# The first half of the first adjacency tile comes in two transfers of 256 columns, and one short warm-up matmul stands where two stood

## The reference, cut to what matters

```
def reference(x, adj, L0_gnn_W, L0_gnn_b):        # x (4096, 256), adj (4096, 4096), W (256, 256)
    h = jnp.maximum(_layernorm(x, axis=-1), 0.0)
    agg = jnp.matmul(adj, h)
    out = jnp.matmul(agg, W.T) + b
    return x + jax.nn.relu(out)
```

## Time and profile before

| | |
|---|---|
| median of 3 runs | 380.52 us (380.36 to 380.57) |
| the profiled execution's own time | 380.32 us |
| its span, first to last instruction | 378.5 us |
| TensorE busy | 375.0 us, 99% of the span |
| VectorE busy | 212.8 us, 56% |
| ScalarE busy | 180.8 us, 48% |
| GpSimd busy | 47.3 us, 13% |
| DMA | 80.25 MB, mean 212 GB/s |

### The profile page before, as it was taken

One profiled execution on the slowest core, in us unless ns is written; L12 is line 12 of the kernel. 1 busy time (PEld: TensorE's weight loads), 2 busy tenths in 40 slices (PEclk: granted clock), 3 DMA queues, 4 the chain that ended last, 5 costly groups with the idle time before them and its releaser, 6 DMA issues.

```text
span 378.5 us, 4516 instructions
## 1 busy us (share of the span) xinstructions
PE 375.0 (99%) x1650; PEld 308.4 (81%) x1650; DVE 212.8 (56%) x295; ACT 180.8 (48%) x227; POOL 47.3 (13%) x88
## 2 busy tenths in 40 slices
PE   9999999999999999999999999999999999999997
PEld 5888888888888888888888888888888888888885
DVE  5999988886444444565564535444464444444424
ACT  4878776765343434543643343434355243434341
POOL 4576732321000000001001000000000100000000
PEclk9999999999999999999999999999999999999999
DMA  7999887658655665556866856565656775656203
GB/s 265 345 314 301 253 300 243 206 193 299 202 192 198 177 210 185 203 175 213 290 207 208 293 178 207 177 208 182 203 187 193 258 240 197 185 204 184 95 2 111
DMA packets 22774, 80.25 MB, mean 212 GB/s; under 512 B 2496, under 2 KB 2880, under 8 KB 22752
## 3 DMA queue, kind: packets, MB, share of 16 engines
q1 hardware_dynamic: 19584, 68.30, 54.5%
q0 software_dynamic: 3168, 11.67, 8.9%
HBM read 75.76 MB, written 4.19 MB: 211 GB/s over the span
## 4 chain that ended last, share of the span: by engine, by line
PE 99%; DVE 0%; issue 0%
PE bank L443 92%; PE bank L486 6%; PE bank L499 1%; DVE out_sb L340 0%
## 5 line engine op out<-in xcount | busy, mean ns | idle before, releaser
L443 PE MATMUL bank<-adj_hi,h_sb 128*128 128x512 f32 x1024 | 254.7, 389 | 0.0
L246 DVE TENSOR_TENSOR adj_lo<-adj_in,adj_hi 128x1024 fp32r<-128x1024 f32 x126 | 154.5, 1226 | 144.2 <-ACT adj_hi L361 144.2
L443 PEld LDWEIGHTS bank<-adj_hi,h_sb 128*128 128x128 f32 x1024 | 192.3, 188 | 40.0 <-ACT h_sb L371 0.3
L361 ACT ACTIVATE adj_hi<-adj_in 128x1024 fp32r<-128x1024 f32 x126 | 133.5, 1060 | 175.9 <-PE bank L443 172.9
L443 PE MATMUL bank<-adj_lo,h_sb 128*128 128x512 f32 x512 | 137.8, 389 | 0.0
L443 PEld LDWEIGHTS bank<-adj_lo,h_sb 128*128 128x128 f32 x512 | 96.1, 188 | 20.0
L238 POOL DMA_DIRECT2D out_t_dram<-out_sb x3 | 2.2, 726 | 205.5 <-DVE out_sb L340 205.5
L220 POOL TENSOR_TENSOR rstd<-var_eps,minus_half 128x1 f32<-128x1 f32 x32 | 27.3, 853 | 4.5 <-DVE var_eps L271 1.9
L371 ACT ACTIVATE h_sb<-centred,rstd 128x256 fp32r<-128x256 f32 x32 | 15.9, 497 | 3.4 <-POOL rstd L220 3.1
L381 ACT ACTIVATE centred<-x_sb,neg_mean 128x256 f32<-128x256 f32 x31 | 15.5, 499 | 3.1 <-DVE neg_mean L286 2.2
L292 DVE SCALAR_TENSOR_TENSOR h_sb<-centred,rstd,h_sb 128x256 fp32r<-128x256 f32 x32 | 15.3, 477 | 0.0
(11 more groups left out here) (26 smaller groups left out, 42.8 us busy)
## 6 DMA issues: line engine op xcount, KB each, us to landing
adj_in<-adj_t_dram SPq DMA_DIRECT2D x126, 512.0 KB, 4.1
xt_sb<-x_t_dram POOLq DMA_DIRECT2D x4, 1024.0 KB, 7.6
x_sb<-x_dram POOLq DMA_DIRECT2D x7, 512.0 KB, 7.1
out_t_dram<-out_sb POOLq DMA_DIRECT2D x3, 1024.0 KB, 4.9
adj_in<-adj_t_dram SPq DMA_DIRECT2D x4, 256.0 KB, 4.5
out_t_dram<-out_sb SPq DMA_DIRECT2D x3, 256.0 KB, 2.0
x_sb<-x_dram POOLq DMA_DIRECT2D x3, 128.0 KB, 6.0
w_sb<-w_t_dram POOLq DMA_DIRECT2D x1, 256.0 KB, 6.6
```

Of the source, the lines that this page charges most:

```text
L246: nc.vector.tensor_tensor(adj_lo[:, k, :], adj_in[:, k, :], adj_hi[:, k, :].bitcast(fp32), ALU.subtract).then_inc(s_lo, 1)
L361: nc.scalar.activation(adj_hi[:, k, :], adj_in[:, k, :], ACT.Copy).then_inc(s_hi, 1)
L443: last = nc.tensor.matmul(bank(g, kb, c)[:], h_sb[:, t, hp, kb * P:(kb + 1) * P], adj_parts[ap][:, n % U, chunk(c)], start=(t == 0 and (hp ...
```

## The change

The first chunk of unit 0, 512 columns, is loaded by two transfers of 256 columns, each with its own semaphore (`s_q`), so the first transfer of adjacency has rows of 1 KB in place of 2 KB, and SyncE issues one transfer more before all that follow. VectorE rounds each quarter of the unit when it has landed. TensorE takes the first pass of the first chunk in four matmuls of 256 columns in place of two of 512, the first two of them when the first quarter has been rounded (`s_quarter`). The second rounded quarter raises the same semaphore `s_hi` that the whole rounded chunk raised before, so ScalarE and VectorE's next steps wait as they did. The two warm-up matmuls of 256 columns behind the first landing become one of 128 columns.

```diff
+    HALF = BANK // 2
+    QUARTERS = (slice(0, HALF), slice(HALF, BANK))
-    WARM_ON = 2
+    WARM_ON = 1
...
             load_x(sp, 0)
-            load_chunk(0, 0)
+            g, t = UNITS[0]
+            for i, cols in enumerate(QUARTERS):
+                at = g * GW + cols.start
+                sp.dma_start(adj_in[:, 0, cols], adj_v[:, t, at:at + HALF]).then_inc(s_q[i], 16)
             load_chunk(0, 1)
...
             def first_rounded():
-                dve.wait_ge(s_early[0][0], 16)
-                nc.vector.tensor_copy(adj_hi[:, 0, chunk(0)], adj_in[:, 0, chunk(0)]).then_inc(s_hi, 1)
+                for i, (cols, made) in enumerate(zip(QUARTERS, (s_quarter, s_hi))):
+                    dve.wait_ge(s_q[i], 16)
+                    nc.vector.tensor_copy(adj_hi[:, 0, cols], adj_in[:, 0, cols]).then_inc(made, 1)
...
+            def first_sums(cols):
+                for kb in range(KB):
+                    nc.tensor.matmul(bank(0, kb, 0)[:, cols], h_sb[:, 0, 0, kb * P:(kb + 1) * P],
+                                     adj_hi[:, 0, cols], start=(cols.start == 0), stop=False,
+                                     skip_group_check=True)
...
                 pe.wait_ge(s_hhi, 1)
-                pe.wait_ge(s_hi, made_chunk(n, 0))
-                add_up(n, [0], 0, 0)
+                if n == 0:
+                    pe.wait_ge(s_quarter, 1)
+                    first_sums(QUARTERS[0])
+                    pe.wait_ge(s_hi, 1)
+                    first_sums(QUARTERS[1])
+                else:
+                    pe.wait_ge(s_hi, made_chunk(n, 0))
+                    add_up(n, [0], 0, 0)
...
-            pe.wait_ge(s_early[0][0], 16)
-            warm_up(WARM_ON, BANK // 2)
+            pe.wait_ge(s_q[0], 16)
+            warm_up(WARM_ON, BANK // 4)
```

More of the change, by code:

```diff
@@ L98, in bass_preln_gnn_residual @@
         s_adj = [sem(f"adj_landed{k}") for k in range(U)]
+        s_q = [sem(f"adj0_quarter{i}_landed") for i in range(2)]
         s_early = [[sem(f"adj{t}_chunk{c}_landed") for c in range(CHUNKS)] for t in range(EARLY)]
@@ L111, in bass_preln_gnn_residual @@
         s_hlo = sem("h_lo_made")
+        s_quarter = sem("first_adj_quarter_made")
         s_hi = sem("adj_hi_made")
```

## The result

| | before | changed |
|---|---|---|
| median | 380.52 us (380.10 to 380.79, 21 runs) | 380.99 us (380.52 to 382.74, 21 runs) |
| ratio to before | | 1.0016 (1.0010 to 1.0022) |
| profiled execution, span | 380.32 us, 378.5 us | 380.99 us, 379.2 us |

The changed kernel is slower by 0.47 us at the median. The time lies inside the stated range, at its upper edge, but the interval of the ratio lies above 1, and the forecast was no change, -0.03. The scatter has grown too, from 0.7 to 2.2 us.

The account below looks back on a forecast made before the run. TensorE was taken to bound the kernel, with only its start and early gates movable. From the 380.52 us median, -0.03 at the rest of adj, +0.00 at the second chunk and an unchanged tail gave 380.5; range 380.2 to 381.0.

Parts of the forecast that it names:

- What bounds the kernel: TensorE: first real matmul's start, a fixed row of matmuls and a short tail; busy 375.0 of 378.5 us.
- The start of real work: First real matmul, released by ScalarE's h at 5.09, starts at about 5.2, 0.27 us earlier than 5.49.
- The matmuls: First pass on TensorE: four of 256 columns for two of 512, +0.03 at full clock; second pass 0.17 us earlier.
- The second quarter: Lands at 4.95 (bounds 4.87 and 5.34); first matmul on adj_lo at about 6.55 against 6.58.
- signs named ahead: Prediction wrong if 512-column matmuls stay 0.43 apart after 7, second cast starts after 5.5, or a later unit makes TensorE wait.
- The transfers behind: Later landings: the DMA queue hides the added 0.47 us issue step; 0.05 is left, taken by 0.2 of slack.
- if nothing hides it: At the second chunk: ScalarE's cast ends at 7.03, not 6.56, and TensorE loses 0.27 us.
- The sum: -0.03 at the gate of the rest of adj, +0.00 at the second chunk, tail unchanged: 380.5 us.
- rival 1: Second quarter, or what is issued behind it, late: +0.2 to +0.6 us, 380.9 in the middle; chance 0.13.
- the rival's second gate: TensorE's wait for the second chunk, at most 0.27 us, overlapping the first gate's 0.36.
- Rival 2, the clock: TensorE's clock rises much later after the shorter warm-up: up to 2.4 us, 382.9; chance 0.06.
- Rival 3, the early start kept: Both quarters land early, first matmul on adj_lo at 6.44, -0.14 us, at best 380.4; chance 0.12.

Follow-up runs that it names:

- the computing alone: Kernel before, first chunk in one transfer, but two casts and four matmuls of 256 columns, old warm-ups: 380.45 us, 1.0001 (0.9992 to 1.0010).
- The tiny transfer: Kernel before with an 8 KB transfer of 128 pieces of 64 bytes added on SyncE behind the first chunk: 380.98 us, 1.0013 (1.0004 to 1.0022).
- the transfers alone: Changed kernel, but both quarters awaited and rounded in one cast, whole-chunk matmuls, old warm-ups: 380.81 us, 1.0019 (1.0007 to 1.0031).
- the warm-ups of before: Changed kernel with the two warm-up matmuls of 256 columns again: 381.15 us, 1.0018 (1.0009 to 1.0026).
- the short one alone: Kernel before with one warm-up matmul of 128 columns in place of two of 256: 380.61 us, 1.0001 (0.9993 to 1.0010).
- the kernel with as many transfers as before: Changed kernel with unit 1's two chunks in one 512 KB transfer: 382.25 us, 1.0048 (1.0035 to 1.0060).
- the last experiment: Kernel before with the rounded h of tile 1 ahead of the rounding of unit 2 on ScalarE: 380.60 us, 1.0005 (0.9996 to 1.0014).

## Why the prediction was wrong

*What bounds the kernel.* Right. TensorE's fixed row and its start decide; from unit 3 on the changed kernel runs as before.

*The start of real work.* Right in its parts. The first quarter landed at 4.2 (taken 4.6, bounds 3.4 and 4.9), its cast took 0.33 as taken, and the first real matmul was let go by ScalarE's `h` and started at 5.07 (predicted 5.2). The 0.13 beyond the prediction is luck: in this execution the first tile of `x` landed 0.15 earlier than in the one of before, and `h` was ready at 4.94 in place of 5.09. Among the kernels in which ScalarE issues no transfer at its start, this landing moves from 2.7 to 3.0.

*The matmuls.* Right: the computing alone gave 1.0001.

*The second quarter.* This is the step that failed first. I let it land at 4.95, and at 5.34 if the issue step were passed on whole. It landed at 5.56, beyond the upper bound, and at 5.1 to 5.5 in the five other kernels in which SyncE issued it, at 1.64. The mean of the six is 5.34, the bound itself: the issue step was passed on whole, and my fault was to take a value near the other end. The reasoning was by bytes: two quarters together are one chunk, so the second can't be much later than the chunk was. The tiny transfer showed that bytes are little of it, since 8 KB in the same place landed at 5.2. One of the signs named ahead, a second cast after 5.5, came true with 5.58. The row to read would have been the second chunk's own: issued at the same 1.65 and landed at 5.9 with 256 KB. By its place the quarter belonged to that transfer, not to the first.

*The transfers behind.* This failed too: "the engines were full from 4.0 on [...] so the issue step is hidden by that queue", and 0.05 for what is left. The full engines were a fact of the old arrangement, not of the chip. With the added transfer the share fell to 0.75, 0.81 and 0.87, and the later landings moved by 0.3 to 0.7 on the mean of the kernels in the table, in the pair shown by up to 1.3. What stood at 0.05 was about the whole issue step. The price "if nothing hides it", 0.27, stopped at the second chunk and left out unit 2. There ScalarE's order makes `h` wait behind the rounding of a late unit, and the slack was 0.39 (ready at 10.50, loaded at 10.89) in an execution in which unit 2 had landed early; it is less than unit 2's mean delay of 0.6. TensorE waiting at a later unit was another of the signs named ahead.

*The sum.* Where -0.03 stood, the profiled execution lost 0.47 by the second matmul on `adj_lo` and 0.65 in all; the rest came in small steps and at unit 2. In the kernels with the transfers alone and with the warm-ups of before, 0.37 and 0.36 were lost by that matmul, and neither waited at unit 2. So in the profiled executions with the change's own order the late second quarter, through VectorE's order, is most of the loss. Its price was somewhat high: by the prediction's sum a cast at 5.58 puts the first matmul on `adj_lo` at 7.18, +0.60, and it started at 6.93, +0.35. The rest of `h` began 0.21 behind the cast (taken 0.28), and after the wait the matmul stood 0.01 behind its weight load (taken 0.20); its successor came 0.34 later in place of 0.22, which gave a part back. It was rival 1 that came true, in sign and size (380.9 forecast, 380.99 measured). I gave it 0.13. That the total agrees so well is in part luck: the rival's second gate, the second chunk, made TensorE wait for nothing in the profiled execution, and unit 2, which did, wasn't in it.

*Rival 2, the clock.* Not the cause of the loss: the warm-ups of before left it where it was, and the short one alone cost nothing at the median. *Rival 3, the early start kept:* the gain at the start was there, 0.42 with the early `x`, and was lost at the second cast.

Open is why the DMA engines, full before, don't hide the issue step of a small transfer added to SyncE's queue, and why units 2 and 3 were late too in the kernel with as many transfers as before. Shown is that the transfer's place in that queue does it and not pieces of 1 KB; that the queue must be SyncE's is not shown. What the DMA engines waited for in the meantime no run tells.

## What to carry to other kernels

At the start of a kernel, ask of a split transfer what its place in the queue costs, not only its bytes: read the landing of the transfer that now has that place, and assume that it will not come earlier. DMA engines that are full in the old trace say nothing of whether they stay full when the issues are cut smaller. And where several gates have slacks of a few tenths of a microsecond, list all that a late transfer reaches, through the order of the engine that waits for it: easing one moved the loss to the next. Last, a landing read from one execution moved by up to 1.0 us in the next kernel with the same queue: compare several before a shift is laid to a change.

## What the runs showed of the hardware

- The place of a buffer changed the pace of every matmul: 229.4 ns in place of 226.9 with `adj_hi` and the other buffers behind it moved by 2,112 bytes per partition, 3.4 us over the kernel, and gone with the extra buffer declared last. Which buffer's place does it wasn't tried.
- A transfer of 8 KB issued behind 256 KB took 3.6 us to land. The Trainium skill's page "DMA: Bandwidth & Descriptors", section "Anatomy of one DMA", would by its fit have about 2.0 us for it, an estimate. The fit is given for transfers that GpSimd issues; for this one, which SyncE issued, the measurement decides.
- TensorE's clock rose at different moments after the same warm-up. In the kernel with the tiny transfer the 256-column warm-up, whose duration was 0.42 at the low level, took

```profile
4.72 0.28 PE L503 MATMUL bank<-const-bfloat16-1.0 128*128 128x256 bf16 x1 [0.24 <-DMA adj_in<-adj_t_dram]
```

and its 512-column warm-ups at 3.88 and 4.10 stand 0.22 apart. So the clock was up before 4 there, about 5.7 in the execution of before and behind 6.3 in those of the short warm-up and of the last experiment. The Trainium skill's page "TensorE: Matmul & The Clock Gate", section "What's actually happening", says that the moment isn't tied to the kernel's start; the traces agree.
- A DMA issue on ScalarE was carried out 1.2 us ahead of the activation that stands before it in the program (0.80 against 2.03). The engine's first work, a table load, ran from 0.73 to 2.01.
- One more semaphore wait at the end of SyncE's program, for a transfer long landed, went with a tail of the kernel 0.1 longer in all five kernels that had it (3.10 to 3.13 from the start of the last matmul, in place of 2.99 to 3.02).
